# Two decoder layers on one core: two of the turned ternary weights copied by ScalarE, the second attention's late maxima over 196 keys, idle products in the first front

## The reference

```
x = LN(x + attention0(x))   # 16 query heads, 4 key heads of 16, rms norm, rotary, causal
x = LN(x + experts_int8(x)) # int8 "smooth" products of x, fside and ctx_1024
x = LN(x + ffn_ternary(x))  # w -> clip(round(w / mean|w|), -1, 1), 256 -> 1024 -> 256, gelu
x = LN(x + attention1(x))   # 16 heads of 16, keys and values from a latent of 64, and the mask
                            #   ((j <= i) & (j >= i - 63)) | ((j < 4) & (j <= i))
x = LN(x + context(x))      # softmax of projected ctx_1024, applied to x
x = LN(x + experts(x))      # 8 experts, top 2, 176 hidden channels
```

## Time and profile before

| what | us |
|---|---|
| median of three runs | 486.82 |
| lowest and highest | 485.5, 491.17 |
| the profiled execution, its own time | 488.25 |
| its span, first to last instruction | 486.5 |
| TensorE busy in the span | 407.2 |
| VectorE busy | 343.8 |
| ScalarE busy | 241.7 |
| GpSimd busy | 111.0 |

### The profile page before, as it was taken

The page is one execution under the profiler, slowest core; times in us unless marked ns, Lnnn a source line. Parts: engine busy times, 40 slices in busy tenths (PEclk is TensorE's granted clock), DMA queues, the critical chain, the costliest instruction groups (busy, mean ns, idle before and its releaser), DMA issues.

```text
span 486.5 us, 8125 instructions
## 1 busy us (share of the span) xinstructions
PE 407.2 (84%) x3100; PEld 311.9 (64%) x3100; DVE 343.8 (71%) x777; ACT 241.7 (50%) x449; POOL 111.0 (23%) x117
## 2 busy tenths in 40 slices
PE   3945677998888656899988689999977899999994
PEld 2515644676665445689556546667766689888883
DVE  2599698777869988656658897657854686666555
ACT  1387703656436967566568415445526334432231
POOL 4500004538511452161570000000005410001001
PEclk9997598999889885899999999999998999999998
DMA  6900020000000000000000019940000000000101
GB/s 192 307 26 1 2 72 4 3 3 3 2 0 2 1 1 0 1 0 2 1 1 1 1 32 113 109 113 4 1 1 0 0 2 1 0 1 0 46 1 43
DMA packets 13126, 13.33 MB, mean 27 GB/s; under 512 B 2904, under 2 KB 12448, under 8 KB 12832
## 3 DMA queue, kind: packets, MB, share of 16 engines
q1 hardware_dynamic: 12224, 12.54, 11.9%
q10 hardware_dynamic: 864, 0.27, 0.2%
HBM read 11.56 MB, written 1.05 MB: 26 GB/s over the span
## 4 chain that ended last, share of the span: by engine, by line
PE 60%; DVE 24%; ACT 7%; DMA 3%; issue 3%; POOL 1%; SPq 0%; ACTq 0%; DVEq 0%; POOLq 0%
PE PS L2377 12%; PE PS L2394 6%; DVE mx L1362 4%; PE PS L2037 3%; PE PS L1953 3%; PE PS L391 3%; PE PS L2078 3%; PE PS L2317 3%; ACT arena L782 3%; PE PS L2301 2%; PE PS L1931 2%; PE PS L2005 2%; DVE arena L1254 2%; DMA arena<-mT 2%; DVE mx L1357 2%
## 5 line engine op out<-in xcount | busy, mean ns | idle before, releaser
L922 ACT ACTIVATE PT<-PS 128x512 f32<-128x512 f32 x96 | 53.5, 594 | 36.4 <-PE PS L2005 36.3
L2377 PE MATMUL PS<-arena_r 128*128 128x512 f32 x264 | 64.6, 393 | 1.4 <-ACT xT L782 1.4
L2377 PEld LDWEIGHTS PS<-arena_r 128*128 128x128 f32 x264 | 48.1, 188 | 11.2 <-issue 2.0
L681 POOL TENSOR_SCALAR va<-mv 128x4 f32<-128x4 f32 x11 | 5.2, 475 | 214.6 <-DVE mv L1179 214.6
L782 ACT ACTIVATE arena<-PS 96x1024 bf16<-96x1024 bf16 (+5 forms) x52 | 39.7, 811 | 19.9 <-PE PS L1931 10.4
L1931 PE MATMUL PS<-ident,arena 128*96 128x128 bf16 x416 | 30.6, 240 | 20.7 <-DVE arena L1244 17.1
L1953 PE MATMUL PS<-masks,ident 128*128 128x512 bf16 x112 | 42.9, 383 | 5.2 <-DVE mx L1362 2.8
L1931 PEld LDWEIGHTS PS<-ident,arena 128*96 128x96 bf16 x416 | 28.4, 139 | 24.8 <-issue 12.2
L1362 DVE TENSOR_REDUCE mx<-PS 128x4 f32<-128x1024 f32 x32 | 39.0, 1220 | 1.1 <-PE PS L1985 0.2
L1357 DVE TENSOR_REDUCE mx<-PS 128x4 f32<-128x512 f32 x32 | 22.0, 687 | 20.1 <-PE PS L1972 20.1
L2394 PEld LDWEIGHTS PS<-arena_r 128*128 128x128 f32 x264 | 34.4, 191 | 1.8 <-DVE arena_r L1734 0.2
(11 more groups left out here) (243 smaller groups left out, 922.0 us busy)
## 6 DMA issues: line engine op xcount, KB each, us to landing
arena<-in_L_ffn_w SPq DMA_DIRECT2D x16, 176.0 KB, 10.6
arena<-in_L_ffn_w SPq DMA_DIRECT2D x2, 1024.0 KB, 11.5
arena<-in_L_ffn_w SPq DMA_DIRECT2D x2, 704.0 KB, 7.4
arena<-in_fside_BxS2xS SPq DMA_DIRECT2D x1, 1024.0 KB, 12.4
out<-x SPq DMA_DIRECT2D x4, 256.0 KB, 2.3
x<-in_x SPq DMA_DIRECT2D x1, 768.0 KB, 8.7
arena<-in_L_attn_Wq SPq DMA_DIRECT2D x2, 256.0 KB, 4.4
arena<-in_L_attn_Wo SPq DMA_DIRECT2D x2, 256.0 KB, 6.0
```

The lines of the kernel that those rows point to most:

```text
L922: nc.scalar.activation(PT[:, n % 2, 512 * j:512 * (j + 1)], bank(3 + j), ACT.Exp, scale=NEG_SCALE)\
L2377: last = mm(bank(2 * (n % 2) + gu), wp[c][:, gu, c_ * P:(c_ + 1) * P], xp[5][:, c, blk * 512:(blk + 1) * 512], start=(step == 0 and c == 0 ...
```

## The change

Four edits, one of them with a change of layout.

1. Of the turned ternary weights, numbers 12 and 14 are copied out by ScalarE, after its third exponentials of the head group; VectorE keeps 11 and 13.

2. The second attention's late maxima take their scores from 196 keys for each head, not 256: keys 64 to 255 and behind them a copy of keys 0 to 3, which `Kh` now holds in four extra columns 256 to 259. Queries 128 to 255 can see no other keys. The mask product now comes last and has 2x192 columns. VectorE's late reduction is over 784 columns.

3. The four extra columns are written by one small copy of 4x4 columns for each of the 16 key groups, ahead of the large one: 12 on VectorE, 4 on ScalarE. The large key copies write four rows of 256 that lie 260 apart. `Kh` grows by 128 words, and what lies behind it moves.

4. TensorE computes products whose result nobody reads, into bank 1: 18 of 128x512 before the transposes of batches 0 and 1 of the first attention, after a wait until VectorE and ScalarE have read tile 5's projection, and 10 before those of batches 2 and 3.

```diff
-        Kh = carve(8192, [P, B, H, S], BF16)
+        SINKS = 4
+        FIRST = 64
+        Kh = carve(8192, [P, B, H, S + SINKS], BF16)
...
+        SHARED = (NGM - B - 3, NGM - B - 1)
...
-            eng_ = "act" if k >= NG2 else "dve" if k in BESIDE or k % 2 else "act"
+            eng_ = "act" if k >= NG2 or k in SHARED else "dve" if k in BESIDE or k % 2 else "act"
...
+        def sinks_beside(b, g):
+            return Kh[0:STK, b, HG * g:HG * g + HG, S:S + SINKS]
+
+        def late_keys(L):
+            return slice(0, S) if L == 0 else slice(FIRST, S + SINKS)
...
                         act.wait_ge(a["stk_tr"], n + 1)
-                        copy(tr_groups(L, b)[g][1], bank16(4 + n % 4, 1024, 0, STK)).then_inc(a["ev_act"], 1)
+                        turned_stack = bank16(4 + n % 4, 1024, 0, STK).rearrange("p (a b) -> p a b", a=HG)
+                        if L == 1 and g < KVH[1] // HG:
+                            copy(sinks_beside(b, g), turned_stack[:, :, 0:SINKS])
+                        copy(tr_groups(L, b)[g][1], turned_stack).then_inc(a["ev_act"], 1)
...
                             exponentials(L, n, 2)
+                        if L == 0:
+                            evac_groups(act, copy, *beside(0, step, g), "act")
...
                 v.tensor_reduce(mx[:, b % 2, 1, HG * g:HG * g + HG],
-                                PS[:, set_ + 1:set_ + 3, :].rearrange("p a (h s) -> p (a h) s", h=2), X, ALU.max)\
+                                PS[:, set_ + 1:set_ + 3, :].rearrange("p a (h s) -> p (a h) s", h=2)
+                                [:, :, 0:late_keys(L).stop - late_keys(L).start], X, ALU.max)\
                     .then_inc(a["mx"], 1)
...
+            def idle_products(bk, n):
+
+                for _ in range(n):
+                    mm(bank(bk), ident16[:, :], masks[:, 0, 0:512], start=True, stop=True)
...
                     pe.wait_ge(w_loaded["tables"], LOADS["tables"])
+                    pe.wait_ge(a["proj_read"], 6)
+                    pe.wait_ge(a["squared"], 6)
+                    idle_products(1, 18)
                     stack_transposes(0, 0)
...
                     last.then_inc(abs_tot, 1)
+                    idle_products(1, 10)
                     stack_transposes(0, 2)
...
-                        if not causal:
-                            mask(bank(bk), slice(P, 3 * P), 2, True)
+                        keys = late_keys(L)
                         for i in range(2):
                             h = HG * g + 2 * j + i
-                            last = mm(bank(bk, S, i * S), Qh[0:STK, b, h, P:S], K_[0:STK, b, kv(h), :],
-                                      start=(causal and i == 0), stop=(not causal and i == 1))
-                        if causal:
-                            last = mm(two_heads(bk)[:, :, P:S], ident16[:, :],
-                                      mk[:, 2 * P:3 * P].unsqueeze(1).to_broadcast([P, 2, P]), start=False, stop=True)
+                            mm(bank(bk, keys.stop - keys.start, i * S), Qh[0:STK, b, h, P:S], K_[0:STK, b, kv(h), keys],
+                               start=(i == 0), stop=False)
+                        lo = P if causal else FIRST
+                        last = mm(two_heads(bk)[:, :, lo - keys.start:S - keys.start], ident16[:, :],
+                                  mk[:, P + lo:3 * P].unsqueeze(1).to_broadcast([P, 2, S - lo]), start=False, stop=True)
                     last.then_inc(a["smax"], 1)
```

More of the change, by code:

```diff
@@ L172, in post_ln_decoder_two_layers @@
         Qh = carve(0, [P, B, H, S], BF16)
-        Kh = carve(8192, [P, B, H, S], BF16)
-        qst = carve(16384, [P, 2, 2 * H * STK], BF16)
-        kst = carve(19456, [P, 2, 2 * H * STK], BF16)
+        SINKS = 4
+        FIRST = 64
+        Kh = carve(8192, [P, B, H, S + SINKS], BF16)
+        qst0 = carve(16384, [P, 2, 2 * H * STK], BF16)
+        qst = carve(16512, [P, 2, 2 * H * STK], BF16)
+        kst = carve(19584, [P, 2, 2 * H * STK], BF16)
         Kh0 = carve(8192, [P, B, KV0, S], BF16)
@@ L180, in post_ln_decoder_two_layers @@
         res4 = [words_of(xb_words, 0, [P, 2, 2, D]), words_of(V1_words, 3072, [P, 2, 2, D])]
-        rem = carve(22528, [P, 2, 2 * 2 * H * HD])
+        rem = [carve(22528, [P, 2, 2 * 2 * H * HD]), carve(22656, [P, 2, 2 * 2 * H * HD])]
         att_words = attT[:, :, :, :].rearrange("p a b c -> p (a b c)")
@@ L210, in post_ln_decoder_two_layers @@
         gwn = carve(18176, [E, D])
-        m1n = carve(16384, [P, 2, EC, D])
-        m2n = carve(22016, [P, DC, E * EI])
+        m1n = carve(16512, [P, 2, EC, D])
+        m2n = carve(22144, [P, DC, E * EI])
         mw1H = [carve_parts(0, [P, 2, EC * P]), carve_parts(2816, [P, 2, EC * P])]
@@ L505, in stack_buffer @@
         def stack_buffer(L, slot, which):
-            buf = qst if which == "q" else (kst0 if L == 0 else kst)
+            buf = ((qst0, kst0), (qst, kst))[L][which == "k"]
             return buf[:, slot % 2, :]
@@ L538, in remainder @@
             o = 0 if which == "q" else 2 * H * HD
-            return rem[:, u % 2, o:o + nh * HD].rearrange("p (h d) -> p h d", d=HD)
+            return rem[L][:, u % 2, o:o + nh * HD].rearrange("p (h d) -> p h d", d=HD)
         def stack_views(L, u, part):
@@ L556, in tr_groups @@
                     srcs = [buf[:, half, h, :] for h in range(HG * g, HG * g + HG) for half in range(2)]
-                    gs.append((srcs, dst[0:STK, b, HG * g:HG * g + HG, :].rearrange("p a b -> p (a b)")))
+                    gs.append((srcs, dst[0:STK, b, HG * g:HG * g + HG, 0:S]))
             return gs
         TG = [KVH[L] // HG + NG for L in range(2)]
+        def sinks_beside(b, g):
+            return Kh[0:STK, b, HG * g:HG * g + HG, S:S + SINKS]
+        def late_keys(L):
+            return slice(0, S) if L == 0 else slice(FIRST, S + SINKS)
         def stack_evac(L, n):
@@ L1253, in evac_stacks @@
                         dve.wait_ge(a["stk_tr"], n + 1)
-                        v.tensor_copy(tr_groups(L, b)[g][1], bank16(4 + n % 4, 1024, 0, STK)).then_inc(a["ev_dve"], 1)
+                        turned_stack = bank16(4 + n % 4, 1024, 0, STK).rearrange("p (a b) -> p a b", a=HG)
+                        if L == 1 and g < KVH[1] // HG:
+                            v.tensor_copy(sinks_beside(b, g), turned_stack[:, :, 0:SINKS])
+                        v.tensor_copy(tr_groups(L, b)[g][1], turned_stack).then_inc(a["ev_dve"], 1)
             def thresholds():
```

## The result

The changed kernel took 480.73 us (median of four runs, 479.43 to 481.01), the kernel before 486.89 (four runs, 485.5 to 491.17). The ratio is 0.99, with a 95% interval of 0.9858 to 0.9941. The profiled execution took 481.01 us, with a span of 479.3 and a mean granted clock of 0.964, against 488.25, 486.5 and 0.940 before. The forecast was 483.0, the range 480.6 to 486.8. All ratios here leave out executions more than 1.5% above the fastest of their kernel and are not quotients of the medians, so the two can differ by some tenths of a per cent.

What follows compares the result with a forecast made beforehand. Bounds: TensorE's clock in the first front; VectorE's reductions, a transfer, then TensorE in the second attention; the first attention's turned weights were judged free. Sum -2.1 + 0 + 0.6 - 1.5 - 0.85 = -3.85, forecast 483.0 us, range 480.6 to 486.8.

Steps and rivals of the forecast that it cites:

- The likeliest single case: The forecast's own case, all terms together: -3.85 us, to 483.0 us; chance 0.42.
- The first front: First attention's start: ten idle products raise the clock for the transposes of batches 2 and 3; -2.1 us, bounds -2.4, +0.2.
- 80 take 5.0 in place of 7.56: Transposes of batches 2 and 3 in the first front: at full clock 5.0 us instead of 7.56.
- Rival B: First front: the clock does not rise for the ten products, or falls again; term 0 or +0.2, 485.1 us; chance 0.25.
- The first set: 18 idle products before the transposes of batches 0 and 1: end in time, any gain hidden by ScalarE's wait; 0 us.
- Two weights on ScalarE: End of the first attention's back: values' product waits for GpSimd, not VectorE; 0 us, bounds -0.5 and +1.2.
- rival E: Move of two turned weights to ScalarE delays exponentials that TensorE waits for: +1.2 us, 484.2 us; chance 0.07.
- Sink copies: Second front: 16 small key copies, partly hidden until batch 2; +0.6 us, bounds 0.2 and 1.9.
- Rival D: Second front's large key copies into four rows lose the fast mode: +2.15 us in all, 489.0 us; chance 0.06.
- Late maxima: Second attention up to step 3: reductions 0.25 us shorter each, gain partly lost at the maxima's transfer; -1.5 us.
- Rival C: Maxima's transfer at step 3 is no bound, first term full, sink copies hidden: -5.85 us, 481.0 us; chance 0.20.
- Step 3: Second attention's step bounded by TensorE: four head groups, each 0.21 us less for shorter mask and score products; -0.85 us.

Runs made afterwards that it cites:

- e3: The kernel before with only the move of two turned ternary weights to ScalarE: 486.41 us, ratio 0.9996.
- e10: The kernel before with only the expert loads reordered (4, 8 and 4 between the transfers of the maxima): 485.62 us, ratio 0.9999.
- e4: The changed kernel without both sets of idle products and without the move to ScalarE, leaving late maxima and sink copies: 483.51 us, ratio 0.9936.
- e2: The kernel before with only the first set of 18 idle products: 484.33 us, ratio 0.9991.
- e1: The kernel before with only the second set of 10 idle products: 483.99 us, ratio 0.9968.
- e8: The changed kernel without the first set of idle products: 481.85 us, ratio 0.9936.
- e5: The changed kernel measured again with no edit, 11 runs: 481.61 us, ratio 0.9924 to the kernel before.
- e6: The changed kernel with 4 expert loads, not 8, between the first and second transfer of the second attention's maxima: 480.05 us, ratio 0.9892.
- e11: The changed kernel with expert loads reordered (4, 8, 4 between the transfers) and without the first set of idle products: 481.46 us, ratio 0.9918.
- e7: The changed kernel with 8 more idle products before the last batch's transposes in the second front: 482.66 us, ratio 0.9947.
- e9: The changed kernel with 20 idle products, not 10, before the transposes of batches 2 and 3: 484.61 us, ratio 0.9971.

## Why the prediction was right, and where it was not

The direction and the range held, and the forecast of -3.85 us lies inside the intervals of both measurements (0.99 and 0.9924, or -4.9 and -3.7 us). The likeliest single case was met by its mechanism. The first median, 480.73, lies 2.3 us under the forecast and 0.1 above the lower end of the range, so that the range held by little.

**The first front, -2.1 forecast.** In the changed kernel -2.35, with the first maxima at 59.28 for a forecast of 59.2. But that number is the best case. From the start of the 80 transposes to the first maxima, the stage lasts 8.54 us before, 8.44 in e3 and 8.48 in e10, but 7.09 in e4 and 6.96 in e2, all five without the second set; with ten products it lasts 7.30 in e1 and e8 and 6.22 in the changed kernel, e5, e6 and e11 (e7, whose transposes start 0.4 us after their input, is left out). The means are 7.9 and 6.6, so the set is worth about 1.3 us, and e1's ratio says 1.6. The step that was mis-sized is "80 take 5.0 in place of 7.56": it sets the coldest case of before against the warmest of after, and each is met only in part of the profiles, three of five and four of six. The sentence that another execution need not fall at the same places was in the prediction, but took only 0.3 off the term. Rival B, that the clock does not rise, came true in part in e1 and e8, where it was down from about 52 to 55.

The Trainium skill ("TensorE: Matmul & The Clock Gate", Part 4: PE-mode transpose) states that transposes do not count as busy for the clock gate. The runs disagree: in e4, in which no products stand ahead of them, 80 bf16 transposes after 4.22 us of idle time took 6.03 us with a mean granted clock of 0.77 from 53 to 59 (0.54 in its first half, 1.00 in its second), so the clock rose under them.

**The first set, 0 forecast.** Nothing speaks against it: 0.9991 alone, and 481.85 without it beside 481.61, both to within about 2 us only. It ended in time even where it began with the clock down: 5.39 us from 30.84 in e5, and the transposes start at 37.01.

**Two weights on ScalarE, 0 forecast.** Confirmed by e3, with the reason given: GpSimd is what the values' product waits for. The changed kernel at this place, GpSimd, ScalarE and TensorE, answers to the earlier trace rows:

```profile
118.74 2.26 POOL L692 TENSOR_SCALAR va<-mv 128x4 f32<-128x4 f32 x1
...
122.80 0.68 POOL L715 TENSOR_SCALAR_AFFINE_SELECT PT<-PT 128x512 f32<-128x512 f32 x1
```

```profile
120.76 1.02 ACT L793 ACTIVATE arena_r<-PS 128x1024 fp32r<-128x1024 bf16 x1
121.68 1.08 ACT L936 ACTIVATE PT<-PS 128x512 f32<-128x512 f32 x2
```

```profile
123.58 1.08 PE L2065 MATMUL PS<-PT,V 128*32 128x256 f32 x8 [1.97 <-ACT PT L936]
```

The copy took 1.02 us (1.1 put), GpSimd's stall of 2.26 is still there, its last select still starts 0.8 before the values' product (125.69 and 126.43 before), and TensorE's wait is 1.97 in place of 1.92. The exponentials slipped and were still in time, so rival E fell.

**Sink copies, +0.6 forecast.** The last batch of the second front in the changed kernel, VectorE, and after it one late reduction:

```profile
268.74 0.16 DVE L1272 COPY arena<-PS 96x16 bf16<-96x16 bf16 x1 [2.03 <-PE PS L1960]
...
274.76 0.97 DVE L1381 TENSOR_REDUCE mx<-PS 128x4 f32<-128x784 f32 x1
```

A small copy took 0.15 to 0.16 us. Between 240 and 264.6 no shift moves by more than 0.05 us, so the copies of the first three batches were hidden altogether; the prediction had batch 2 on the chain as well. From 264.6 to 277.8 the shift goes back by 0.4 to 0.6 in e4 to e8, 0.2 of it while the last batch's keys are copied. In the changed kernel's own profile it is 1.8, since there VectorE waited 2.03 us for cold transposes (granted clock 0.72 in 266 to 272, above). In e9 and e11 it is 1.8 and 1.7, with the clock at 0.58 and 0.59 in 270 to 274; but it is 1.5 in e10 too, which has no small copy, so the fall is not theirs. Rival D fell: the key copies into four rows took 0.68 us, as the contiguous ones did. This agrees with the Trainium skill ("VectorE: DVE Perf Modes", What auto-detection actually checks), which asks of such a copy only 16-bit tensors with step 1.

**Late maxima, -1.5 forecast up to the transfer.** The reduction took 0.97 us (970 ns forecast), and from 277.8 to 292.0 the shift grows by 1.96 or 1.97 in the changed kernel, e4, e5, e6, e8 and e11, where 1.95 was forecast (by less in e7 and e9). Of that and of TensorE's share a part was to be lost at the transfer, and was. The chain of waits of the changed kernel answers to the earlier trace rows:

```profile
287.57 0.17 PE PS L2013 x2
287.74 0.17 PE PS L2016
...
290.09 10.97 DMA arena<-mT
```

TensorE's pieces fell from 0.22 to 0.17 us each. The transfer was issued 6.5 us earlier and took 10.97 us in place of 10.28. TensorE waited 1.4 us for it. Net, from 277.8 to 306.9, the shift grows by 1.47 where 1.5 was forecast, and by 1.3 to 1.7 in e4, e5 and e8. e6 shows the cap by removing it: 3.0 us in the same stretch. Rival C, that the transfer is no bound, fell, although its number, 481.0, is next to the median.

**Step 3, -0.85 forecast.** From 306.9 to 360.0 the shift grows by 0.83 in e4 and e8, in steps of 0.21, but by 0.63 in the changed kernel and 0.51 in e5, which lose 0.2 to 0.3 against these two between 315 and 320; why stays open.

**The sum.** The stages that the change edits give -2.35 + 0 + 0.4 - 1.5 - 0.6 = -4.05 in the changed kernel, taking the sink copies as in most other runs; the forecast was -3.85. With 1.3 for the first front, as the means of the profiles have it, the sum is -3.0. The interval of the second measurement, -5.3 to -2.0, holds both, so that the nearness of -3.85 to its -3.7 is in part luck. The other 3.2 of the 7.2 us between the two first profiles belong to no edit: they are the steps of 0.6 between 61.6 and 138, of 1.6 and 1.6 up to 199.6 and of 0.75 after 360, less 1.4 in the second front. The step of 1.6 from 138.2 to 145.4 is in the changed kernel, e2 and e4 to e9, and not in e1, e3, e10 and e11, and no one edit divides them so. That an edit upstream makes the one place likelier than another was not shown. Against the median the sum was also made from an uncertain base: the prediction took one profiled execution and three runs as the kernel's level, but with 35 runs the kernel before spreads from 482.53 to 491.47, and its median stood anywhere from 484.7 to 486.9 between jobs. That the base and four runs of the changed kernel account for the 2.3 us is likely and not shown.

## What to carry to other kernels

Filling an idle stretch with products that nobody reads pays only just before TensorE-bound work, and only up to the moment at which that work could start: ten were worth 1 to 2 us here, twenty lost most of it, and eighteen ahead of work that VectorE bounds gave nothing that the times show. When a stage gets quicker, look at which transfer is issued in it and what stands in front of that in the queue; moving four loads behind it was worth 0.2 us in its stage before and 1.7 us after. Before pricing a gain in clock from one profile, compare stage lengths over several profiles: the same transposes took 7.55 and 6.03 us with nothing changed around them.

## What the runs showed of the hardware that was not expected

- The granted clock falls at different places in executions that have the same instructions there: 0.57 or 1.00 in 141 to 145, 0.50 or 0.77 in 53 to 59. Late falls of 1.2 to 1.6 us each came at 348 to 354 in e6 and at 363 to 378 in e1.
- Idle products at full clock do not always keep it. In e1 and e8 TensorE was idle for 2.04 us after them and the clock was down under the first transposes; in e6 and e11 the same idle time stood there and it stayed at 1.00 (transposes 2.43 + 2.40 us).
- A second spread, of 1.7 to 2.6 us, lies in the first projections, far ahead of any edit. The chain of waits of the changed kernel, and that of its repetition e5, each with its window from 14 to 18 (in brackets the products that ran in it):

```profile
14.16 4.53 PE PS L1892 x8
...
14.00:18.00 4.00, 4.00 (x8) 1.00 0.98 329
```

```profile
13.79 2.79 PE PS L1892 x8
...
14.00:18.00 4.00, 4.00 (x13) 1.00 0.98 318
```

  The same eight products took 4.53 and 2.79 us in the same program. They took 2.79 in e1, e5, e6 and e8, whose second run of transposes starts 1.5 to 1.9 us earlier than before, and 4.53 to 5.43 in all others, the kernel before among them. The trace says that this is the clock's first rise, although the windows show 1.00: in the changed kernel successive products of one projection start 0.64 us apart up to 17.46 and 0.32 us apart from 17.87 on, exactly half; in e5 they are 0.32 apart from the second on. The trace's first clock record starts at 17.6 and at 13.1, and in e7, the slowest, at 19.6. So a window ahead of the first clock record shows 1.00 although the products in it run at half the pace. What decides the place of the rise was not tried.
- A transfer of 8 KB took 10 to 11 us from issue to landing when it was issued 1.3 to 2.3 us after eight loads of 176 KB, and about 2 to 3 us when it was issued 3.2 to 4.2 us after four. How much of this is the number of loads and how much the distance in time was not tried.
